# Turning three tiles by VectorE block transposes and DMAs through DRAM instead of TensorE transposes, in an AdaLN attention-and-MLP kernel

## What is computed

```python
h = layernorm(x) * (1 + ca) + sa
x = x + ga * attn(h)            # ca, sa, ga, cb, sb, gb: one row of 256 per sequence
h = layernorm(x) * (1 + cb) + sb
x = x + gb * ffn(h)
# attn: 4 heads of 64, chunks of C = 64 tokens, the chunks of a sequence one after the other
rk = unit-length rows of h per head;  wk = rk of the token before;  v = h @ Ww.T
A = inv(I + strict(wk @ wk.T) * L)    # L: powers of the head's decay
v_new = A @ v - (A @ wk) @ S
o = (rk * gp) @ S + (strict(rk @ wk.T) * L) @ v_new
S = gamma_C * S + (wk * gp_tail).T @ v_new
attn(h) = h + (alpha * o) @ Wr.T
# ffn: 256 -> 1024 (silu gate) -> 1024 (gelu) -> 1024 (gelu) -> 256, weights in {-1, 0, 1} times a scale
```

## Time and profile before

| what | value |
|---|---|
| median of 3 runs | 1741.35 us (1739.12 to 1741.45) |
| the profiled execution | 1740.26 us, its span 1738.4 us |
| TensorE busy | 1710.8 us, 98% |
| VectorE, ScalarE, GpSimd busy | 63%, 56%, 34% |
| granted TensorE clock, mean | 0.991 |

### The profile page before, as it was taken

One profiled execution on the slowest core, in us unless ns is written; L12 is line 12 of the kernel. 1 busy time (PEld: TensorE's weight loads), 2 busy tenths in 40 slices (PEclk: granted clock), 3 DMA queues, 4 the chain that ended last, 5 costly groups with the idle time before them and its releaser, 6 DMA issues.

```text
span 1738.4 us, 60948 instructions
## 1 busy us (share of the span) xinstructions
PE 1710.8 (98%) x25488; PEld 1645.9 (95%) x25488; DVE 1100.7 (63%) x3137; ACT 965.3 (56%) x2249; POOL 593.5 (34%) x694
## 2 busy tenths in 40 slices
PE   8799999999999999999999999999999999999999
PEld 5699999999999999999999999999999999999998
DVE  5677666666666666666666666666666666666432
ACT  4664555555555555555555555555555555555554
POOL 3544333243333243333243333243333243333111
PEclk8899999999999999999999999999999999999999
DMA  8201000000000000000000000000000000000000
GB/s 273 87 17 30 12 23 23 18 21 14 22 23 24 17 21 11 24 23 24 18 20 13 22 23 23 17 21 14 21 23 23 17 21 17 18 23 17 6 4 14
DMA packets 37360, 47.12 MB, mean 27 GB/s; under 512 B 9236, under 2 KB 29336, under 8 KB 37080
## 3 DMA queue, kind: packets, MB, share of 16 engines
q1 hardware_dynamic: 35088, 40.75, 8.5%
q10 hardware_dynamic: 1992, 2.38, 0.5%
HBM read 22.53 MB, written 8.39 MB: 18 GB/s over the span
## 4 chain that ended last, share of the span: by engine, by line
PE 93%; ACT 1%; DVE 1%; POOL 1%; issue 1%; DVEq 0%; ACTq 0%
PE mlp L1153 64%; PE mlp L1225 6%; PE solo L1153 3%; PE duo L1421 3%; PE solo L1294 3%; PE solo L1126 2%; PE duo L1342 1%; PE duo L1119 1%; PE duo L1410 1%; PE duo L1315 1%; PE duo L1114 1%; PE solo L1430 1%; PE solo L1136 1%; PE duo L1412 1%; PE duo L1306 1%; PE duo L1277 1%
## 5 line engine op out<-in xcount | busy, mean ns | idle before, releaser
L1153 PE MATMUL mlp<-act_hi,w_hi 128*128 128x256 f32 x4096 | 968.9, 283 | 1.1 <-POOL act_lo L654 0.6
L1153 PE MATMUL mlp<-act_lo,w_hi 128*128 128x256 f32 x4096 | 946.3, 277 | 0.2 <-issue 0.2
L1153 PEld LDWEIGHTS mlp<-act_hi,w_hi 128*128 128x128 f32 x4096 | 769.8, 188 | 10.1 <-POOL act_lo L654 1.4
L1153 PEld LDWEIGHTS mlp<-act_lo,w_hi 128*128 128x128 f32 x4096 | 770.2, 188 | 1.3 <-issue 0.4
L791 ACT ACTIVATE full<-mlp,scale_sb 128x256 f32<-128x256 f32 x512 | 246.7, 482 | 554.2 <-PE mlp L1153 554.0
L881 DVE TENSOR_TENSOR act_lo<-full,act_hi 128x256 fp32r<-128x256 f32 x512 | 240.6, 470 | 339.2 <-ACT act_hi L792 336.3
L654 POOL TENSOR_TENSOR act_lo<-full,act_hi 128x256 fp32r<-128x256 f32 x256 | 186.8, 735 | 493.4 <-ACT act_hi L781 493.4
L792 ACT ACTIVATE act_hi<-mlp,scale_sb 128x256 fp32r<-128x256 f32 x512 | 243.9, 476 | 0.0
L1153 PE MATMUL mlp<-xh,w_hi 128*128 128x256 f32 x768 | 185.7, 282 | 4.3 <-issue 3.4
L1153 PE MATMUL mlp<-xl,w_hi 128*128 128x256 f32 x768 | 184.9, 281 | 0.0
L593 POOL TENSOR_TENSOR rstd<-ve,minus_half 128x2 f32<-128x2 f32 x64 | 48.7, 761 | 335.4 <-DVE ve L830 335.0
(11 more groups left out here) (178 smaller groups left out, 2660.9 us busy)
## 6 DMA issues: line engine op xcount, KB each, us to landing
w_raw<-in_wts SPq DMA_DIRECT2D x22, 512.0 KB, 5.4
kg<-r SPq DMA_DIRECT2D x64, 126.0 KB
xin<-in_x SPq DMA_DIRECT2D x62, 128.0 KB
out_y<-y SPq DMA_DIRECT2D x62, 128.0 KB, 2.5
step_and_inv<-square_t SPq DMA_DIRECT2D x56, 64.0 KB, 2.0
wmod_sb<-in_wmod ACTq DMA_DIRECT2D x1, 1024.0 KB, 9.6
kg<-last SPq DMA_DIRECT2D x64, 2.0 KB
last<-r SPq DMA_DIRECT2D x64, 2.0 KB, 1.7
```

What stands on the lines that cost most here:

```text
L1153: mm = pe.matmul(dst, *general_ops, start=is_first and i == 0, stop=is_last and i == 1)
```

## The change

The transposes of `start` and `turn` leave `mixed`. In their place VectorE turns each 128x512 tile in 32x32 blocks (`flip` 0 for `h`, `flip` 1 for `r`, `turn` for `xn2`), and the blocks get to their places by DMA: four DMAs write the four groups of 32 partitions to a DRAM tensor, in pieces of 512 bytes, and when they have landed one DMA reads it back with whole rows. That is 15 DMAs a step more, all issued by SP. The tiles `hT`, `rT`, `rg` and `head_decay` have the four blocks innermost, so that neighbours of a block are 16 bytes apart. `near`, `cross` and `o_state` hold the turned blocks on their way out and `vn` the turned `xn2`. The flips are made one walk ahead, in l2, and read after column 1 of the next l3. In the list `stats` goes ahead of `lead`, `unit` from l2's column 5 to 4, `residual` from the end of l2 to column 2 of the next l3, `norm2` and `turn` to the head, and `fs` and `expand` one place forward. Column 0 of l3 makes its last product after the first three of column 1.

```diff
+BETWEEN = 3
+SQ = 32
+SQS = P // SQ
+    h_dram, r_dram, x_dram = (nc.dram_tensor(k, (SQS, SQ, SQS, NP * SQ), F32, kind="Internal").ap() for k in ("h_squares", "r_squares", "x_squares"))
-    rT = [sb(f"rT{i}", [NP, 2, C + 1]) for i in range(2)]
+    rT = [sb(f"rT{i}", [2, C + 1, NP]) for i in range(2)]
-    hT = sb("hT", [KT, NB, P])
+    hT = sb("hT", [P, NP])
-    rg = sb("rg", [NP, 2, C])
+    rg = sb("rg", [2, C, NP])
-    mixed = listed([("rg", 0, 0), ("start", 0, 1)], late + layers[:2 * HK], {
-        ("l3", 0): [("norm2", 0, 0)],
-        ("l3", 1): [("values", 0, 1), ("pred", 0, 0), ("gram", 0, 1), ("turn", 0, 0), ("intra", 0, 1), ("u", 0, 0)],
-        ("l3", 2): [("fs", 0, 1)],
...
+    mixed = listed([("rg", 0, 0), ("norm2", 0, 0), ("turn", 0, 0)], late + layers[:2 * HK], {
+        ("l3", 1): [("values", 0, 1), ("pred", 0, 0), ("gram", 0, 1), ("intra", 0, 1), ("u", 0, 0), ("fs", 0, 1)],
+        ("l3", 2): [("fs", 1, 1), ("residual", 0, 1)],
...
-        ("l1", 7): [("lead", 0, 0), ("far", 0, 1), ("stats", 0, 2)],
-        ("l2", 0): [("old", 0, 0), ("norm", 0, 2)],
+        ("l1", 7): [("stats", 0, 2), ("lead", 0, 0), ("far", 0, 1)],
+        ("l2", 0): [("old", 0, 0), ("norm", 0, 2), ("flip", 0, 2)],
         ("l2", 1): [("keys", 0, 0)],
         ("l2", 2): [("join", 0, 0), ("square", 0, 2)],
         ("l2", 3): [("length", 0, 2)],
-        ("l2", 4): [("n", 3, 1), ("state", 0, 0)],
-        ("l2", 5): [("unit", 0, 2)],
-        ("l2", 6): [("attn_out", 0, 0), ("residual", 0, 2)],
+        ("l2", 4): [("n", 3, 1), ("unit", 0, 2), ("state", 0, 0), ("flip", 1, 2)],
+        ("l2", 6): [("attn_out", 0, 0)],
+    def by_square(blocks):
+        return blocks.rearrange("p (c n q) -> p c q n", c=SQS, n=SQ)
+            def move_normed(n):
+                sp.wait_ge(xn2_turned, n - 2)
+                spread_squares(x_blocks, x_dram, xn2_out)
+                sp.wait_ge(xn2_out, SPREAD * n - 2 * SPREAD)
+                sp.dma_start(x_turned, x_dram.rearrange("c p i n -> (c p) (i n)")).then_inc(x_in_turned, 16)
+            def spread_squares(blocks, dram, done):
+                for i in range(SQS):
+                    sp.dma_start(dram.rearrange("c p i n -> p c i n")[:, :, i, :], blocks[SQ * i:SQ * i + SQ].rearrange("p (c n) -> p c n", c=SQS)).then_inc(done, 16)
+            def move_blocks(a, p):
+                sp.wait_ge(v_full, a)
+                sp.wait_ge(h_turned, a - 3)
+                spread_squares(h_blocks, h_dram, h_out)
+                sp.wait_ge(h_out, SPREAD * a - 3 * SPREAD)
+                sp.dma_start(hT[:].rearrange("p n q -> p (n q)"), h_dram.rearrange("c p i n -> (c p) (i n)")).then_inc(hT_in, 16)
+                sp.wait_ge(pred_full, a - 2)
+                sp.wait_ge(rg_ready, a - 2)
+                sp.wait_ge(r_turned, a - 3)
+                spread_squares(r_blocks, r_dram, r_out)
+                sp.wait_ge(r_out, SPREAD * a - 3 * SPREAD)
+                sp.dma_start(rT[p][:, :, 1:C + 1, :].rearrange("p c n q -> p c (n q)"),
+                             r_dram.rearrange("c p i n -> (c p) (i n)").rearrange("p (c m) -> p c m", c=2)).then_inc(rT_in, 16)
...
+                if items in (third, mixed) and (whole or n + 2 < STEPS):
+                    move_blocks(n + 2, g)
...
+                    if name == "flip" and k == 0:
+                        dve.wait_ge(h_ready, now)
+                        dve.transpose(by_square(h_blocks), h[:].rearrange("p b (k c n) -> p c (b k) n", k=KT, n=SQ)).then_inc(h_turned, 1)
...
-                return pe.matmul(duo[1][half(1 - e), b, col:col + C], state[half(e), q, c, :], rg[half(e), q, c, :], start=True, stop=True)
+                return pe.matmul(duo[1][half(1 - e), b, col:col + C], state[half(e), q, c, :], rg[half(e), c, :, q], start=True, stop=True)
...
+                    if paired and k == 0:
+                        layer("l3", 0, range(HK - 1))
+                    if paired and k == 1:
+                        layer("l3", 1, range(BETWEEN))
+                        layer("l3", 0, range(HK - 1, HK))
+                        layer("l3", 1, range(BETWEEN, HK))
...
                         if items is mixed:
-                            pe.wait_ge(rT_ready, n + 1)
+                            pe.wait_ge(hT_in, MOVES * n - 2 * MOVES)
+                            pe.wait_ge(rT_in, MOVES * n - 2 * MOVES)
+                            pe.wait_ge(diag_ready, n + 1)
+                            pe.wait_ge(rT_ready, now)
...
-                                mm = pe.matmul(solo[0][:, b * D:(b + 1) * D], hT[:, kt, b, :], wv_sb[:, kt, :], start=kt == 0, stop=kt == KT - 1)
+                                mm = pe.matmul(solo[0][:, b * D:(b + 1) * D], hT[:, :, b * KT + kt], wv_sb[:, kt, :], start=kt == 0, stop=kt == KT - 1)
...
-                            mm = pe.matmul(grams(a, e)[half(c), q, :], rT[p][half(e), q, c, 0:C], rT[p][half(e), q, c, :], start=True, stop=True)
+                            mm = pe.matmul(grams(a, e)[half(c), q, :], rT[p][half(e), c, 0:C, q], rT[p][half(e), c, :, q], start=True, stop=True)
```

More of the change, by code:

```diff
@@ L338, in main @@
         ("l2", 1): [("solve", 1, 0), ("fs", 3, 1), ("expand", 0, 1), ("stats", 0, 2)],
-        ("l2", 2): [("state", 0, 0), ("norm", 0, 2)],
+        ("l2", 2): [("state", 0, 0), ("norm", 0, 2), ("flip", 0, 2)],
         ("l2", 3): [("far", 0, 1), ("n", 1, 1), ("square", 0, 2)],
-        ("l2", 4): [("length", 0, 2), ("attn_out", 0, 0), ("residual", 0, 2)],
-        ("l2", 5): [("n", 2, 1), ("unit", 0, 2)],
+        ("l2", 4): [("length", 0, 2), ("attn_out", 0, 0)],
+        ("l2", 5): [("n", 2, 1), ("unit", 0, 2), ("flip", 1, 2)],
         ("l2", 7): [("n", 3, 1)],
@@ L534, in step @@
                 whole = not isinstance(n, int)
-                if items is mixed and (whole or n + 1 < STEPS):
-                    attention(n + 1, 1 - g)
+                if items is mixed and (whole or n <= STEPS):
+                    move_normed(n)
                 if whole or 2 <= n <= STEPS + 1:
@@ L540, in step @@
                         load_last(n - 1)
+                    if items is mixed and (whole or n + 1 < STEPS):
+                        attention(n + 1, 1 - g)
                     if items is third:
@@ L901, in part @@
                         dve.wait_ge(rT_full, now)
[L903 to L905 removed]
+                        dve.tensor_copy(rT[p][:, :, 0, :], rT[1 - p][:, :, C, :])
+                        dve.tensor_copy(rT[p][:, :, 1:C + 1, :].rearrange("p c n q -> p q c n"), turned_r(a).rearrange("p (q c n) -> p q c n", q=NP, c=2)).then_inc(rT_ready, 1)
+                    if name == "flip" and k == 0:
+                        dve.wait_ge(h_ready, now)
+                        dve.transpose(by_square(h_blocks), h[:].rearrange("p b (k c n) -> p c (b k) n", k=KT, n=SQ)).then_inc(h_turned, 1)
+                    if name == "turn" and items is mixed:
+                        dve.wait_ge(xn2_ready, n)
+                        dve.transpose(by_square(x_blocks), xn2[:].rearrange("p k b (c n) -> p c (k b) n", n=SQ)).then_inc(xn2_turned, 1)
+                    if name == "flip" and k == 1:
+                        dve.wait_ge(r_ready, now)
+                        dve.transpose(by_square(r_blocks), r[:].rearrange("p b (k c n) -> p c (b k) n", k=KT, n=SQ)).then_inc(r_turned, 1)
+                        dve.tensor_copy(rT[p][:, :, 0, :], rT[1 - p][:, :, C, :]).then_inc(rT_ready, 1)
                     if name == "keys":
@@ L1044, in heads @@
                         row_pow = solo[1][half(e), e * NPAIR * C:(e + 1) * NPAIR * C].rearrange("p (q n) -> p q n", n=C)
-                        ins = dve.tensor_copy(head_decay[half(e), :, c, :], row_pow)
+                        for b in range(NB):
+                            ins = dve.tensor_copy(head_decay[half(e), c, :, b * NPAIR:(b + 1) * NPAIR].rearrange("p n q -> p q n"), row_pow)
                 ins.then_inc(heads_ready, 1)
@@ L1285, in part @@
                             pe.wait_ge(tables_ready, 1)
-                        pe.wait_ge(hT_ready, now)
+                        if items is not mixed:
+                            pe.wait_ge(hT_ready, now)
                         if items in (second, third):
@@ L1309, in part @@
                         pe.wait_ge(const_in, 16)
-                        pe.wait_ge(hT_ready, now if items is alone else begun(n, items))
-                        pe.wait_ge(rT_ready, now if items is alone else begun(n, items))
+                        if items is mixed and isinstance(n, int):
+                            pe.wait_ge(ao_scaled, n)
+                            pe.wait_ge(state_ready, n)
+                        if items is not mixed:
+                            pe.wait_ge(hT_ready, now if items is alone else begun(n, items))
+                            pe.wait_ge(rT_ready, now if items is alone else begun(n, items))
                         if items is alone:
@@ L1423, in part @@
                         mm.then_inc(ao_full, 1)
```

(2 more changed lines are left out.)

85 lines of the change are left out of this document (49 added, 36 removed), and 4 rows, old and new, of the table mixed.

## The result

The changed kernel takes 1795.53 us (median of 4 runs, 1794.24 to 1797.3), the kernel before on the same chip 1740.23 (1738.07 to 1741.45): a ratio of 1.032, interval 1.0302 to 1.0338. It is slower by 55 us. The forecast of 1708 and the range to 1756 both missed, on the other side of no change. The span of the profiled execution is 1795.5 us.

A forecast was written before the change was run, and what follows sets the result against it. TensorE, busy 98% of the span, was taken as the bound. 1740.3 - 36.9 (transposes) + 3 (stride) = 1706.4, with the median 1.1 above that execution 1707.5, said as 1708; range 1702 to 1756 for 8 in 10.

The forecast's parts named there:

- Added to TensorE: the stride: Values, prediction, gram and old state read fp32 operands 16 bytes apart; cost taken as 3 us, range 0 to 39.
- the ratio: TensorE's strided reads: a port slowed by 1.6 still suffices, so the stride costs nothing, plus 3 us for values loads.
- read at VectorE's rate: Closing condition: the prediction is wrong if TensorE reads fp32 operands 16 bytes apart at 1.86 ns an element.
- The absolute reading: TensorE's four strided groups pay 1.86 ns an element: some 1.4 us a step, 39 us, a time near 1743.
- Taken from TensorE: Transposes removed from mixed: 28 steps of 0.88 us for start, 30 of 0.41 for turn, saving 36.9 us.
- No wait: MLP input's DMA road at ScalarE's ln2: data there about 807, wanted at 807.9, so nothing is lost.
- neither engine is the bound, and I take nothing for them: ScalarE's copy of hT and VectorE's of rT go too; no gain counted.
- The order of l3: Column 0 with 20 matmuls put ahead gets act_lo block 7 0.7 us before need; cost zero, old order 0.0 to 0.2.
- VectorE: Three 128x512 block transposes a step at 0.7 to 1.1 us each, 2.1 to 3.3 us, hidden in idle time.
- The roads: Two DMA hops through DRAM take 6.5 to 8.2 us with waits; keys have 0.2 to 2.3 us of slack.
- the keys arrive late: Rival, 12%: second hop takes 5 us or more, TensorE stands 2 us before the values in 28 steps; 1760.
- the stride eats the gain: Rival, 20%: absolute rate on four strided groups plus some quadrant contention, 1.4 to 1.8 us a step; taken 1749.

The follow-up runs named there:

- dense: Changed kernel, but the DMAs land in near and cross, and ScalarE and VectorE copy into layouts with adjacent elements; 1729.84 us, ratio 0.9936.
- b_16bytes: Kernel before, TensorE transposes kept and no DMA added; only hT, rT, rg, head_decay get four blocks innermost, 16 bytes apart; 1807.35 us, ratio 1.0384.
- dense_keys: Changed kernel, keys and input copied to adjacent layouts, keys earlier in one step, MLP input turned by TensorE, ln2 reading PSUM; 1730.21 us, ratio 0.9956.

## Why the prediction was wrong, step by step

**The step that failed** is "Added to TensorE: the stride", where two prices stood and I took the ratio. The ratio argued that fp32 asks for an element each 0.88 ns and a port slowed by 1.6 still gives one each 0.71. The runs show an absolute rate: 128 columns of the values' load take (936.24 - 934.19) / 8 = 256 ns, 2.0 ns an element, and a prediction's 64 columns 4 x 31 = 125 ns over four quadrants, 1.95 ns. The reason for which I preferred the ratio ("its rows are TensorE's own") is no reason: those rows were of adjacent elements. VectorE's 1.86 ns was near, but partly by luck. That row read 32 bytes apart and summed groups of 8; VectorE's copy that does read 16 bytes apart (dense, 764 ns for 512) comes, with the same 165 ns off, to 1.17 ns an element. So the last line of the prediction, "read at VectorE's rate", names no rate that the runs confirm. The absolute reading had 1.4 us a step; 1.99 were measured, because the old state pays 0.73 and not 0.42 (its 32 unchanged partners do not hide it), prediction and gram 1.02 for 0.83, and the values 0.24 for 0.1. The 28 steps that I counted were too few too: the first steps have the strided groups as well, but keep their transposes. b_16bytes puts all of it, with 0.2 us a step that l2 and l3 take more there, at 67 us against the upper bound of 39, and dense takes 66 back.

**Taken from TensorE** held: 1.206 us a step for the 0.79 and 0.41, and 0.08 for the 0.09 of the MLP's resumption, which hides in the row of l2 and l3.

**ScalarE** failed as well. "No wait" for the MLP's input was right for the DMA, which is issued at 938.69, lands 2.4 us later and is used at 946.65. But I costed the arrival and not the reading: 0.37 us a half on an engine whose idle time per column is 0.97, right ahead of the last `act_hi` on which y waits. The sum has no term for it, and where the prediction speaks of ScalarE's work ("neither engine is the bound, and I take nothing for them") it reads a share of 56% as slack; in the last three columns of l3 ScalarE has none. The size is 0.55 us a step in the changed kernel, and 0.55 again between dense and dense_keys.

**The order of l3**: cost zero was predicted. Columns 0 and 1 take 0.1 us a step more by their starts, not counting the saved resumption, and 0.2 in dense; no row names what they wait for. **VectorE**: 1.09 to 1.13 us a block transpose, at the upper end given. **The roads**: 3.1 + 3.2 us for the keys where I had 6.5 to 8.2 with waits, 2.3 us of slack in the steady steps, the rival "the keys arrive late" wrong there. In the first walk of `mixed` it was right once, in a list (`third`) whose order I did not cost.

**The rival** "the stride eats the gain" had mechanism and side right, at 20%, and its sum (1749) was short by 46 us. It also named contention between the quadrants, which no run separates from the stride.

**The 13 us before step 5 and the 4 at the end.** The values of steps 3, 4 and 5 start at 145.0, 172.6 and 224.4 us in the kernel before, at 148.3, 176.2 and 230.7 in b_16bytes, and at 151.2, 182.0 and 237.3 in the changed one. So 6.3 of the 13 us are the strides, 3.7 the late road and the lower clock behind it, and 2.9 are lost before that. The 4 us at the end are the strides as well: from the values of step 31 to the end it is 159.8 us before, 160.1 in dense, 163.4 in b_16bytes and 163.9 in the changed kernel.

**What stays open** is the 2.9 us. They go with the jump into the main program near 60 us, where TensorE waits 6.9 us without a releaser for 3.4 before. b_16bytes has 3.5 there, dense 4.8 in two waits, and dense_keys, which has no road for the MLP's input, 3.6. Why is not shown. Open too are the 2 ns between starts in l3 and the 0.1 us of its first columns.

## What to carry to other kernels

Moving a transpose off TensorE changes the layout in which its operand lies, and the operand's reader pays for that. fp32 operands 16 bytes apart cost TensorE about 2 ns an element here; for fp32 operands like these pack at most two tiles into neighbouring words, or copy once into a dense tile on engines that have time (here 28 copies each by ScalarE and VectorE turned +3.2% into -0.6%, and ScalarE's cost at most 2 us). And read the slack of a side engine in the columns just ahead of the join where it is awaited, not as a share of the span.

## What was not expected of the hardware

Writing 16 bytes apart has a price as well. With the same source in PSUM, ScalarE's copy into `hT` takes 1086 ns in b_16bytes where it took 588 before, and VectorE's into `rT` 1072 where it took 683. Reading 16 bytes apart costs ScalarE 1123 ns in dense, where its copies from PSUM take 586 (that source differs in memory too). VectorE's read, also from SBUF, takes only 764 ns. ScalarE in before and b_16bytes, VectorE in b_16bytes, and both in dense:

```profile
L739 ACT COPY hT<-duo 128x512 f32<-128x512 f32 x31 | 18.2, 588 | 0.4 <-PE duo L1277 0.4
L738 ACT COPY hT<-duo 128x512 f32<-128x512 f32 x31 | 33.7, 1086 | 0.4 <-PE duo L1281 0.4
L905 DVE COPY rT<-duo 128x512 f32<-128x512 f32 x31 | 33.2, 1072 | 0.0
L786 ACT COPY hT<-near 128x512 f32<-128x512 f32 x28 | 31.4, 1123 | 0.0
L960 DVE COPY rT<-cross 128x512 f32<-128x512 f32 x28 | 21.4, 764 | 10.1 <-DMA cross<-r_squares 10.1
```

And the road is short: 64 KB written to DRAM in pieces of 512 bytes land in 1.8 us, 256 KB read back in 2.7, so that two hops take 6 us, less than the 7.6 us of the one transfer of 279 KB among the first loads.
